# Four-layer graph network on one core: transposed x kept in SBUF as quarters, pair sums made in place, weight sums in three buffers

## The reference

```python
# layer 1: gated GCN, four rounds with tanh gates, on x1 = x @ W1 + b1 (512 wide)
gnn_out = gnn_out + _graph_gcn(gnn_out, row, col, gate_w[kk], gate_b[kk], n_nodes)
# layer 2: GraphSAGE, twice, with two pairs of 1024x1024 weights
return h @ W_self + mean @ W_neigh + b
# layer 3: graph attention
h = x @ W
h_prime = jax.ops.segment_sum(e[:, None] * h[dst], src, num_segments=N)
# layer 4: GCN with self loops and symmetric norm
h = x @ W
out = jax.ops.segment_sum(msg, dst, num_segments=n) + b
```

## Time and profile before

| | us |
|---|---|
| median of three runs | 1686.04 |
| fastest, slowest | 1683.31, 1690.53 |
| the profiled execution, whole | 1690.04 |
| its span, from first to last instruction | 1688.2 |

### The profile page before, as it was taken

The page is one execution under the profiler, slowest core; times in us unless marked ns, Lnnn a source line. Parts: engine busy times, 40 slices in busy tenths (PEclk is TensorE's granted clock), DMA queues, the critical chain, the costliest instruction groups (busy, mean ns, idle before and its releaser), DMA issues.

```text
span 1688.2 us, 19851 instructions
## 1 busy us (share of the span) xinstructions
PE 1521.5 (90%) x6685; PEld 1203.4 (71%) x6685; DVE 1033.9 (61%) x1652; ACT 800.0 (47%) x1498; POOL 404.4 (24%) x457
## 2 busy tenths in 40 slices
PE   8999999999678869999779779987999999879997
PEld 6877778788456647877557558766788778657775
DVE  9878898876347445554446455556589356245655
ACT  7676657677223324544123324344487246433332
POOL 0111252434443130001451320012144013320012
PEclk9999999999889989999889889998999999989998
DMA  5343374248987664547986664356656247783435
GB/s 193 112 156 105 109 239 140 95 145 283 315 280 250 234 214 159 191 151 231 288 301 233 233 212 130 127 177 231 197 161 201 92 169 273 254 261 124 143 91 176
DMA packets 152564, 324.03 MB, mean 192 GB/s; under 512 B 27202, under 2 KB 67772, under 8 KB 149896
## 3 DMA queue, kind: packets, MB, share of 16 engines
q1 hardware_dynamic: 139486, 283.87, 51.9%
q10 hardware_dynamic: 12970, 38.77, 6.0%
HBM read 221.76 MB, written 100.82 MB: 191 GB/s over the span
## 4 chain that ended last, share of the span: by engine, by line
PE 41%; DMA 24%; DVE 13%; ACT 8%; POOL 6%; issue 5%; SPq 2%; ACTq 1%; DVEq 0%; POOLq 0%
PE bank L1259 8%; PE bank L1263 6%; PE bank L1261 6%; DMA Ar<-a_d 5%; DMA xs_d<-U 3%; DMA sr_d<-U 3%; PE bank L1095 3%; PE bank L1096 3%; PE bank L1097 3%; DMA xs<-xs_d 3%; PE bank L1270 3%; PE bank L1126 2%; PE bank L1127 2%; PE bank L1128 2%; ACT Tt L1434 2%
## 5 line engine op out<-in xcount | busy, mean ns | idle before, releaser
L1259 PE MATMUL bank<-Zh,Mh 125*125 125x512 f32 x990 | 401.0, 405 | 3.5 <-DVE Zl L1831 3.2
L1126 PE MATMUL bank<-wh,xh 128*125 128x512 f32 x700 | 299.7, 428 | 114.4 <-DVE xl L1762 99.1
L1762 DVE TENSOR_TENSOR xl<-xs,xh 128x500 fp32r<-128x500 f32 (+1 forms) x205 | 168.7, 823 | 340.8 <-ACT xh L1399 339.0
L1399 ACT CAST xh<-xs 128x500 fp32r<-128x500 f32 (+1 forms) x205 | 137.0, 669 | 412.8 <-DMA xs<-xs_d 185.1
L1127 PE MATMUL bank<-wl,xh 128*125 128x512 f32 x700 | 291.9, 417 | 0.0
L1128 PE MATMUL bank<-wh,xl 128*125 128x512 f32 x700 | 290.9, 416 | 0.0
L1126 PEld LDWEIGHTS bank<-wh,xh 128*125 128x125 f32 x700 | 140.4, 201 | 167.9 <-issue 126.7
L1270 PE MATMUL bank<-Zl,Mh 125*125 125x512 f32 x590 | 238.5, 404 | 19.6 <-DVEq L1773 19.5
L1259 PEld LDWEIGHTS bank<-Zh,Mh 125*125 125x125 f32 x990 | 187.3, 189 | 49.6 <-ACT Zh L1469 4.1
L1128 PEld LDWEIGHTS bank<-wh,xl 128*125 128x125 f32 x700 | 139.8, 200 | 36.9
L1127 PEld LDWEIGHTS bank<-wl,xh 128*125 128x125 f32 x700 | 140.9, 201 | 33.1
(11 more groups left out here) (228 smaller groups left out, 2567.4 us busy)
## 6 DMA issues: line engine op xcount, KB each, us to landing
Ar<-a_d SPq DMA_DIRECT2D x100, 312.5 KB, 3.0
xs<-xs_d SPq DMA_DIRECT2D x100, 250.0 KB, 5.3
x_d<-XO ACTq DMA_DIRECT2D x30, 512.0 KB, 4.4
R<-x_d SPq DMA_DIRECT2D x60, 256.0 KB
xT_d<-XT ACTq DMA_DIRECT2D x30, 500.0 KB, 4.0
Tt<-ws_d SPq DMA_DIRECT2D x52, 256.0 KB, 5.7
xs<-xT_d SPq DMA_DIRECT2D x45, 250.0 KB, 6.2
ws_d<-U SPq DMA_DIRECT2D x10, 1024.0 KB, 4.9
```

Source lines behind the costliest of these rows:

```text
L1126: te.matmul(o, xh[b][:, 4 * h + k, :], wh[s][:], start=(k == 0 and not onto), stop=False, skip_group_check=True)
L1259: te.matmul(o, Mh[i][:, s, :], zh, start=(n == 0), stop=False)
L1762: ve.tensor_tensor(xl[b][:, part, :], xs[b][:, part, :], xh[b][:, part, :].bitcast(f32), ALU.subtract) \
```

## The change

x is no longer fetched for each job. Twenty quarter tiles (`QUART`) rest in SBUF, in the memory of `Zh` and `Zl`, during `self` of layers 1 and 2; another 25 (`QUART4`, for `zq` of layer 4) lie in `G`, `GW`, `XT`, `xs` and `XO`. In layers 1 and 4 the transposed tiles are copied from PSUM straight into them; in layer 2 SyncE loads 20 quarters from `hT_d`, at most two in a turn, none before job 139 is done. `first` and `second` read the resting quarters (`x_of`), so no load is issued for those jobs, except P1 and P2 of `self` 2. GpSimd makes the x sums in place, one quarter at a time (`pair_sum`). Since `zq` of the same layer writes over parts of them, S1 and S4 alone are stored to HBM and loaded again for P5 and P3. `zq` of layers 1 and 2 still loads X11, X12 and X22.

Weight sums: the 20 steps stay, but each has a turn of its own for the load, for each of the four sums and for the store, and there is a third place, `GW`. Five steps stand in the gate jobs (four before).

`second` of `mean` and `loop` jobs from the third tile on is called two turns ahead, in `lower`.

In `steps`, a row is: place, turn of the load, turns of the four sums, turn of the store, product, k step.

```diff
+def loads_x(job):
+    if job.kind == "self":
+        return job.layer == 2 and job.phase in ("P1", "P2")
+    return job.kind != "zq" or job.layer < 3 and job.phase not in ("P6", "P7")
...
-    steps += [(at["zq", 1] + 2 + 3 * k, "w", 2, k) for k in range(4)]
+    g, z = LAST_GATE, START["self", 1]
++    steps = [(1, g - 16, (g - 15, g - 14, g - 13, g - 12), g - 11, 0, 0),
...
+             (0, z + 3, (z + 5, z + 6, z + 7, z + 8), z + 9, 1, 2),
...
+    for p, z in ((2, START["zq", 1]), (4, START["zq", 2])):
+        steps += [(1, z, (z + 3, z + 4, z + 5, z + 6), z + 7, p, 0),
+                  (1, z + 10, (z + 13, z + 14, z + 15, z + 16), z + 17, p, 1),
+                  (1, z + 21, (z + 25, z + 25, z + 26, z + 26), z + 27, p, 2),
+                  (1, z + 29, (z + 30, z + 30, z + 31, z + 31), z + 32, p, 3)]
...
+for _p in SUM_STARTS:
+    for _i in range(HT):
+        _t = START[_p] + (9 + _i if _p[0] == "self" else 2 + 3 * _i // 2)
+        XSUMS += [(_t, _p[1], _f, _i) for _f in ("S1", "S3", "S2")]
+        XSUMS.append((START[_p] + 20 + _i, _p[1], "S4", _i))
...
-        PW = [U3F[:], XB[:].rearrange("p (q c) -> p q c", q=4)]
+        PW = [U3F[:], XB[:].rearrange("p (q c) -> p q c", q=4), GWL.rearrange("p (q c) -> p q c", q=4)]
...
+            def quarter_load(k, i):
+                q.wait_ge(s_mm, START["self", 2])
+                sy.dma_start(QUART[k][i], x_source(2, k // 2, i, k % 2)).then_inc(d_xr[k][i], 16)
...
+                    if not loads_x(job):
+                        return
...
-                    ac.copy(XT[x % 2][:, 4 * n:4 * n + 4, :], bank[b][:, 0:4 * T].rearrange("p (a c) -> p a c", c=T)) \
-                        .then_inc(s_te, 1)
+                    elif f == 0:
+                        ac.copy(QUART[2 * (job.d // HT) + n][job.d % HT], src).then_inc(s_te, 1)
...
-                    elif JOBS[i].kind in ("gate", "att", "kept"):
+                    elif JOBS[i].kind in ("gate", "att", "kept") or JOBS[i].kind in ("mean", "loop") and JOBS[i].d >= 2:
                         second(i)
...
-                if j + 1 < NJ and JOBS[j + 1].kind in ("mean", "loop"):
+                if j + 1 < NJ and JOBS[j + 1].kind in ("mean", "loop") and JOBS[j + 1].d < 2:
                     second(j + 1)
...
+            def pair_sum(n):
...
+                    po.tensor_tensor(s1, x21, x22, ALU.add).then_inc(s_sx, 1)
...
+                    po.tensor_tensor(x21, x11, x21, ALU.subtract).then_inc(s_sx, 1)
```

More of the change, by code:

```diff
@@ L429, in same_bank_before, with stored_count @@
     return next((k for k in range(i - 1, -1, -1) if GROUP_BANK[k] == GROUP_BANK[i]), None)
-STORES = [j for j in range(NJ) if any(w not in ("row", "rows", "wc") for _, w, _ in GROUPS[j])]
+STORES = [j for j in range(NJ) if finishes(j) != 2 and any(w not in ("row", "rows", "wc") for _, w, _ in GROUPS[j])]
 WC_GROUPS = [i for j in range(NJ) for i, w, _ in GROUPS[j] if w == "wc"]
 STORE = {j: i for i, j in enumerate(STORES)}
+def stored_count(i):
+    return sum(16 * (1 + (finishes(STORES[k]) == 0)) for k in range(i % 2, i + 1, 2))
@@ new lines, in step_before, with step_nth @@
+def step_before(n):
+    return next((i for i in range(n - 1, -1, -1) if STEPS[i][0] == STEPS[n][0]), None)
+def step_nth(n):
+    return sum(o[0] == STEPS[n][0] for o in STEPS[:n + 1])
+SUM_STARTS = (("self", 1), ("self", 2), ("zq", 4))
+XSUMS = []
+for _p in SUM_STARTS:
[3 more added lines that the diff above has]
+        XSUMS.append((START[_p] + 20 + _i, _p[1], "S4", _i))
@@ L731, in bank_free, with x_of, x_landed @@
                 q.wait_ge(s_post, PI[o] + 1)
+        def x_of(j):
+            job, (b, h) = JOBS[j], divmod(X_SLOT[j], 2)
+            if not job.phase:
+                return xs[b][:]
+            if loads_x(job):
+                return xs[b][:, 4 * h:4 * h + 4, :]
+            k = 4 if job.layer == 4 and job.phase == "P5" else X_PLACE[job.phase]
+            return resting(job.layer, k, job.d).rearrange("p (k n) -> p k n", k=4)
+        def x_landed(q, j):
+            job = JOBS[j]
+            if loads_x(job):
+                q.wait_ge(d_xs[X_SLOT[j]], 16 * X_NTH[j])
+            elif job.phase in X_SUM:
+                sum_made(q, job.layer, X_SUM[job.phase], job.d)
+            else:
+                rested(q, job.layer, X_PLACE[job.phase], job.d)
         def slab_split(q, g):
@@ L844, in step_load @@
             def step_load(n):
-                t, what, p, i = STEPS[n]
-                if n >= 2:
-                    step_stored(q, n - 2)
-                else:
+                place, turn, _, _, p, k = STEPS[n]
+                if n == 0:
                     build_over(q)
-                dst = PW[n % 2]
-                if n % 2 == 0:
-                    u3_free_of_products(q, t)
-                elif what == "x" and p == 1:
+                if step_before(n) is not None:
+                    step_stored(q, step_before(n))
+                if place == 0:
+                    u3_free_of_products(q, turn)
+                elif place == 2:
+                    q.wait_ge(s_post, PI[J0[2] + NT - 1] + 1)
+                elif p == 2:
                     for d in range(NT - 2, NT):
@@ L867, in step_load @@
[L867 to L877 removed]
+                dst = PW[place]
@@ L1532, in apply @@
                 if i in (0, 1, NT, NT + 1):
-                    for n in range(len(STEPS)):
-                        if STEPS[n][0] < j and n % 2:
-                            step_stored(q, n)
+                    free_of_steps(q, 1, j)
                 if f == 2:
@@ new lines, in tail @@
+                    n += 1
+                if n == 0 or f == 2:
+                    return
+                x = STORE[j]
+                q.wait_ge(s_te, GROUPS[j][-1][0] + 1)
+                if f == 0:
+                    if x >= 2:
+                        stored(q, STORES[x - 2])
+                    for k in range(2):
+                        ac.dma_start(xT_d[1][job.d][:, k * QX:(k + 1) * QX], QUART[2 * (job.d // HT) + k][job.d % HT]) \
+                            .then_inc(d_xt[x % 2], 16)
+                    return
@@ L1600, in attention_row @@
+                if f is None:
+                    h = job.half
+                    dst = hT_d[job.d].rearrange("p (k n) -> p k n", k=8)[:, 4 * h:4 * h + 4, :]
+                else:
+                    dst = xT_d[f + 1][job.d].rearrange("p (k n) -> p k n", k=8)
+                ac.dma_start(dst, XT[x % 2][:, 0:4 * n, :]).then_inc(d_xt[x % 2], 16)
             def attention_row(j):
@@ L2417, in rsqrt_degrees, with weight_sum @@
                     .then_inc(s_deg, 1)
-            def four_sums(n):
-                t, what, p, i = STEPS[n]
-                v = PW[n % 2]
-                s11, s12, s21, s22 = (v[:, k, 0:QX if what == "x" else HW] for k in range(4))
-                q.wait_ge(d_pl[n % 2], 32 * (n // 2 + 1))
-                if what == "w":
+            def weight_sum(n, m):
+                place = STEPS[n][0]
+                s11, s12, s21, s22 = (PW[place][:, k, :] for k in range(4))
+                mine()
+                if m == 0:
+                    q.wait_ge(d_pl[place], 32 * step_nth(n))
```

246 lines of the change are left out of this document (161 added, 85 removed).

## The result

The changed kernel takes 1546.24 us (median of 4 runs, 1544.77 to 1551.16), the kernel before 1686.8 (1683.31 to 1690.53) beside it: ratio 0.9171, 95% interval 0.9142 to 0.9201, so 140 us faster. The profiled execution took 1547.23 us, with a span of 1545.4 against 1688.2. By the two profiled executions it is 142.8 us, 22 less than the sum had. The forecast was 1524 us with 1500 to 1592 as its ends, so 1546 lies inside, 22 us above the middle.

The account below looks back on a forecast made before the run. TensorE was taken as held by late x transfers behind weight stores in SyncE's queue, plus the lower clock that follows; 165 + 12 + 4 won less 16 charged, 1690 - 165 = 1525, stated as 1524 us, range 1500 to 1592.

Parts of the forecast that it names:

- the sum: Whole kernel: 181 us won less 16 us charged, net 165 us off the profiled 1690.0 us.
- What bounds the kernel: Three product stretches lose 165 us: 110 us of TensorE waits for late x transfers, about 55 us of lower clock.
- x from resting quarters: `self` 1 and `zq` 4: no x loads before products; x sums just fit in `self` 1, 3 us charged, ends 0 and 8.
- the quarter loads: `self` 2: the only added transfers in a tight place, close to issue and bandwidth limits; 4 us charged, ends 0 and 12.
- Weight sums far ahead: `zq` 1 and 2: 5 us stalls go, 2 us charged over both, ends 0 and 6; gates: nothing charged, bad end 10.
- VectorE beside GpSimd: Product stretches: VectorE needs 2.3 us a product beside GpSimd's sums, under the 2.8 available; nothing charged.
- the first rival: All stages: a third of the gain returns through VectorE and GpSimd's shared path, 45 us, giving 1569 us; chance 0.13.
- Mean and loop products: Earlier `second` ends `sem_inc` waits: 12 us won in `mean` 2's second half, 4 us in other `mean` and `loop` jobs.
- The ring of the earlier trace: `mean` 2, 1101 to 1177: edge block's release, 3.78 us load, split, slab's cast, then VectorE's turn to the next release.
- The slower rival: Gate turns and stage starts: 20 weight-store holds of 8.9 us reach TensorE, 178 us, giving 1702 us; chance 0.03.

## Why the prediction was right, and where it was off

**What bounds the kernel: right.** The waits at the first quarter matmul were a matter of transfers, and the low clock went with them. Of 165 us lost in the three product stretches 66.1 + 58.2 + 26.0 = 150.3 came back.

**x from resting quarters: the mechanism right, the charges met by luck.** GpSimd's first S1 of `self` 1, in time order:

```profile
447.62 1.57 POOL L2602 TENSOR_TENSOR XR<-XR 128x500 f32<-128x500 f32 x1 [1.91 <-DVE xl L1907]
```

That is 30.6 us behind the stage's start at 417, as forecast ("about 30"). It waits 1.91 us for `second` of the quarter it overwrites, which the prediction hadn't named. No long wait followed: 0.4 us before the first product of P6 and less than 0.25 before the last, where the 3 us were charged. The stretch has 4.1 us idle all the same, 2.3 of them at the 41st product, behind the x load shown above. `self` 2 with `zq` 2 has 4.6 us for the 4 charged to the quarter loads, and those show no cost at all: the 1.16 us before its second product follow the last R load of `mean` 1 (12.04 us from 726.99 on), while the first quarter load is issued at 741.37, and in the run with the steps in `self` 2 the first 15 products have no wait over 0.25 us. The rest is the 2.83 us at 856. `zq` 4 has no idle time, as charged.

**Weight sums far ahead: right where it looked, wrong where it didn't.** In `zq` the store no longer holds x loads: in `zq` 1 SyncE waited there for GpSimd for 44.5 us before and not at all after. This part alone is worth 60 us (weights at their old turns). The step that failed is the charge: "2 us over both" and, for the gates, "nothing charged". The prediction weighed the load against its own sums and the store against its sums, and never asked who is queued behind the load in `mean` 1. It cost 14.6 us there and 3 in the gates, 13.7 counting what was there before; in `zq` 1 and 2 themselves the two waits at the 41st product, 5.1 us, stand for the 2 charged. Six kernels show that this cost can be moved, and none that it can be removed: where whole steps moved, 11 to 15 us came free in one stage and 11 to 13 were paid in the next.

**VectorE beside GpSimd: charged at nothing, and its true size stays open.** The means rose (xl to 0.876, wl to 1.228), and with the sums shrunk the kernel is 18 us shorter. So GpSimd's sums do cost something, about 18 us by this run, 1% of the kernel. How much of it goes over VectorE isn't shown: the mean per product stayed under its bound, 0.88 + 0.69 + 0.8 x 1.23 = 2.55 us, TensorE hardly waits for `second`, and the waits that went away stood behind SyncE's loads. The Trainium skill, "SBUF — State Buffer", section "SBUF: two separate sides", says that the two engines' port pair is locked by one of them for a whole instruction; the two-operand forms at 876 and 1228 ns against 671 and 791, with the PSUM form at 687 and 688, agree with it. What it would make at its worst, the first rival's 1569 us, did not come: TensorE waits 0.5 us for `second` in `self` 1.

**Mean and loop products: the wait named went, half of its worth came.** 13.7 us for `sem_inc` in `mean` 2 became 0.6, as forecast. The stage won 5.2 us of 12, and the first `z` stage behind it gave 2.4 back: it takes 60.5 and 61.0 us in the two traces without the early call and 62.2 or more in the twelve with it. The ring of the earlier trace rows stayed, and TensorE meets it elsewhere: ScalarE waits for the edge block (22.9 us), and the copy to PB, for which the transposes wait, stands behind it. The prediction asked when the wait ends, and not what is late next. Over all stages the early call is worth 14 us of the 16 forecast, twice measured; in the `loop` and `mean` stages outside this one it gave more than its 4 us (4.0 in `loop` and 3.1 in `mean` 1, by the kernel with the old weight turns). In the kernel with the early call alone, 4 of the 12 us that its span is shorter lie in `self` 2 and `zq` 4, which have no such jobs; where they come from is open.

**The slower rival** took SyncE's holds at weight stores as passed on to TensorE. They are there, and a cost with them, but about 14 us in each of two stages (gates and `mean` 1), 10 of it there before, and not 8.9 for each of 20 steps.

**The sum.** 165 less 142.8 is 22 us missing. 14.6 are the steps in `mean` 1 and 7 the missing part of `mean` 2; gates (3.0) and `z` (2.4) are about made up by the 3.1 us of `mean` 1 without its steps and by the product stretches, which lost 1.3 less than charged. The low clock behind each short wait is in all of these.

**Still open.** How the 18 us of GpSimd's sums divide between VectorE and SyncE's queue. A third buffer for the edge block, which would break the ring in `mean` 2, and smaller step loads (a quarter of 250 KB in turn, with the short loads between them) were not tried. No kernel here that makes all its sums is shown to be faster than the changed one: the lowest, with `zq` 2's weight steps earlier (0.9111), lies inside the interval of the changed kernel's second run (0.9085 to 0.918).

## What to carry to other kernels

An operand that is used again and fits in SBUF can be worth more than the bytes it saves, as here: its loads no longer stand in a queue with stores that wait for another engine, and the clock stays up. "Far ahead" frees the transfer itself, not those behind it: before a bulk load is moved, list what is next in its queue in the new place, how long a short load takes behind it, and who waits for that. When a release is moved earlier, look for the next engine in the same ring; half of the wait may stay under another name.

## What the runs showed of the hardware

A load of about 250 KB that stood near a step's 1 MB load or store in the queue took 8.6 to 12.3 us to land (R 8.63, 9.35, 12.04 and 12.25, xs 9.29, 9.46 and 10.99). In the second half of `mean` 1 the edge block, 312.5 KB, took 7.0 us in the median with the steps in that stage and 4.5 with them moved out. With them the stage moved 274 GB/s, under the 306 of the page's highest slice, so a rate below the highest doesn't mean that short transfers are quick. And the long gate products hid less than I had thought: the gates went from 304.3 to 290.6 us, at a clock of 1.00, when the two steps at their end were taken out and the stores of the others came a turn or two later.
